# Gathering the rows of batches 4 to 7 in four groups between the stages of an embedding and attention kernel

## What is computed

```python
def _L0_tok_ref(token_ids, base_embeddings, rule_transform, token_rules):
    base_embeds = base_embeddings[token_ids]
    rule_indices = token_rules[token_ids]
    rule_matrices = rule_transform[rule_indices]
    return jnp.einsum('bsd,bsde->bse', base_embeds, rule_matrices)
...
h = _L0_tok_ref(x, L0_tok_base_embeddings, L0_tok_rule_transform, L0_tok_token_rules)
h = h + _L0_attn_ref(_layernorm(h, axis=-1), L0_attn_Q, L0_attn_K, L0_attn_VO)
h = h + _L0_ffn_ref(_layernorm(h, axis=-1), L0_ffn_Wg, ..., L0_ffn_b2)
```

## Time and profile before

| | us |
|---|---|
| median of 3 runs | 663.07 |
| lowest, highest | 662.15, 665.81 |
| the profiled execution | 663.97 |
| its span, first to last instruction | 662.2 |

### The profile page before, as it was taken

One profiled execution on the slowest core, in us unless ns is written; L12 is line 12 of the kernel. 1 busy time (PEld: TensorE's weight loads), 2 busy tenths in 40 slices (PEclk: granted clock), 3 DMA queues, 4 the chain that ended last, 5 costly groups with the idle time before them and its releaser, 6 DMA issues.

```text
span 662.2 us, 9427 instructions
## 1 busy us (share of the span) xinstructions
PE 526.7 (80%) x2732; PEld 291.5 (44%) x2732; DVE 419.1 (63%) x1018; ACT 288.0 (43%) x566; POOL 230.6 (35%) x379
## 2 busy tenths in 40 slices
PE   0173903697879379699999999999999899999684
PEld 0043801255644133344544554454454455666462
DVE  5621686563115166588868886896975866764566
ACT  0101401035554144445565556556555445466333
POOL 5674057623225710040134133223322413454422
PEclk9995965569799569799999999999999989999968
DMA  8732513813472106252422142044043100000000
GB/s 245 266 88 50 129 35 78 195 39 95 97 207 41 26 7 151 54 124 58 97 51 48 42 92 69 1 97 104 2 97 79 27 1 10 1 11 8 2 8 9
DMA packets 21935, 47.05 MB, mean 71 GB/s; under 512 B 6264, under 2 KB 11720, under 8 KB 21824
## 3 DMA queue, kind: packets, MB, share of 16 engines
q1 hardware_dynamic: 15552, 32.23, 20.5%
q0 software_dynamic: 4752, 8.20, 4.9%
q10 hardware_dynamic: 1584, 6.03, 2.8%
HBM read 9.97 MB, written 11.01 MB: 32 GB/s over the span
## 4 chain that ended last, share of the span: by engine, by line
PE 55%; DVE 18%; issue 9%; DMA 5%; another core or an unknown queue 4%; ACT 4%; POOL 3%; SPq 2%; DVEq 0%; ACTq 0%; POOLq 0%
PE bank L1217 13%; PE bank L1203 10%; PE bank L1183 6%; PE bank L1075 5%; PE bank L1145 4%; DVE mx L952 4%; PE bank L1167 4%; PE bank L1139 2%; PE bank L1140 2%; DVE r_sb L999 2%; POOL r_sb L586 1%; DMA front<-in_weights 1%; PE bank L1228 1%; POOL ctxT L517 1%
## 5 line engine op out<-in xcount | busy, mean ns | idle before, releaser
L952 DVE TENSOR_REDUCE mx<-bank 128x1 f32<-128x512 f32 x256 | 171.5, 687 | 111.1 <-PE bank L1203 84.4
L586 POOL TENSOR_TENSOR r_sb<-r_sb 128x256 f32<-128x256 f32 x180 | 93.9, 521 | 280.4 <-DVE r_sb L1017 176.6
L643 ACT ACTIVATE prob<-bank 128x512 f32<-128x512 f32 x256 | 139.0, 596 | 74.7 <-PE bank L1183 43.8
L1203 PE MATMUL bank<-ks,qs 96*128 96x512 f32 x256 | 124.7, 491 | 25.6 <-DVE mx L952 12.4
L1217 PE MATMUL bank<-prob,xa 128*64 128x512 f32 x448 | 125.3, 638 | 2.8 <-issue 2.8
L1203 PEld LDWEIGHTS bank<-ks,qs 96*128 96x128 f32 x256 | 51.4, 201 | 144.3 <-issue 122.9
L1183 PE MATMUL bank<-qs,ks 97*128 97x512 f32 x224 | 79.0, 435 | 0.8 <-DMA qs<-negm 0.8
L701 ACT ACTIVATE r_sb<-bank,stay 128x512 f32<-128x512 f32 x56 | 37.1, 687 | 44.9 <-PE bank L1140 44.6
L1075 PE MATMUL bank<-r_sb,eT 128*64 128x64 f32 (+1 forms) x544 | 44.4, 242 | 12.3 <-ACT eT L626 8.3
L1075 PEld LDWEIGHTS bank<-r_sb,eT 128*64 128x64 f32 x544 | 39.4, 154 | 19.6 <-issue 10.6
L1183 PEld LDWEIGHTS bank<-qs,ks 97*128 97x128 f32 x224 | 39.1, 196 | 16.8 <-issue 10.8
(11 more groups left out here) (159 smaller groups left out, 700.7 us busy)
## 6 DMA issues: line engine op xcount, KB each, us to landing
qs<-qk_h SPq DMA_DIRECT2D x64, 128.0 KB
ks<-qk_h SPq DMA_DIRECT2D x56, 128.0 KB
qs<-qk_l SPq DMA_DIRECT2D x32, 128.0 KB
ks<-qk_l SPq DMA_DIRECT2D x28, 128.0 KB
emb_sorted<-front ACTq DMA_DIRECT2D x4, 608.0 KB
y_sorted<-y_out POOLq DMA_DIRECT2D x19, 128.0 KB, 2.4
e_in<-emb_sorted POOLq DMA_DIRECT2D x9, 256.0 KB, 3.3
emb_sorted<-front ACTq DMA_DIRECT2D x3, 640.0 KB
```

Of the source, the lines that this page charges most:

```text
L586: nc.gpsimd.tensor_tensor(a[:, at:at + width], src[:, 0:width], src[:, width:2 * width], ALU.add).then_inc(S["pool_chain"], 1)
L643: nc.scalar.activation(prob[:, step % NPROB, u % 2, :], bank[u % NST][:], ACT.Exp, scale=SC).then_inc(S["exp_done"], 1)
L952: V.tensor_reduce(mx[:, u // 16, u % 16:u % 16 + 1], bank[3 + n % 2][:], AX.X, ALU.max).then_inc(S["mx_done"], 1)
L1203: M(bank[3 + n % 2][:], qs[0:96, nb % 2, h, tt * 128:(tt + 1) * 128], ks[0:96, nb % 2, h, :], start=True, stop=True).then_inc(S["s_ps"], 1)
```

## The change

Batches 2 and 3 are gathered where all six were. The rows of batches 4, 5, 6 and 7 are gathered at the start of stages 1, 2, 3 and 4, four transfers each, in front of the copy of values of that stage.

```diff
             for g in range(TOTAL - 4, TOTAL):
                 store_sent(pool, g)
-            for b in range(2, B):
-                bring(1, b)
+            bring(1, 2)
+            bring(1, 3)
             n = 0
...
             for b in range(-2, B + 1):
+                if 1 <= b and b + 3 < B:
+                    bring(1, b + 3)
                 if 2 <= b + 2 < B:
                     values(b + 2)
                 for k in range(16):
```

## The result

| | before | after | ratio of the two |
|---|---|---|---|
| median | 664.44 us, 4 runs (662.15 to 669.08) | 649.14 us, 4 runs (643.64 to 656.62) | 0.9731, interval 0.9678 to 0.9784 |
| profiled execution | 663.97 us (span 662.2) | 656.62 us (span 654.8) | |

The median fell by 15.3 us, where 12.6 was forecast from a median of before of 663.07. The profiled run of after is the slowest of its four and counts as slow, so the ratio leaves it out, and its whole span says little; it is read by stretches. (Lines after the change stand two lower: L952 is now L954, L1203 is L1205, L1217 is L1219, L1122 is L1124.)

What follows compares the result with a forecast made beforehand. DVE, ACT and PE were taken to stand idle on late words from PE during the row of 24 gathers. Gains 9.6 + 3 = 12.6 us; 663.97 - 12.6 = 651.4, median 0.9 lower: 650.5 us, range 643.5 to 661.

Steps and rivals of the forecast that it cites:

- The place and the mechanism: Row of 24 gathers: after some seven, PE's words to DVE and ACT come late, until at most 4 us after the last.
- The 9.6 us: Gain up to batch 2's transposes, starting at about 226 instead of 235.65, because the row ends at its eighth gather.
- both bouts: Two spells of late PE words beside the 24 gathers; the first, to 218.16, was expected to stay.
- nothing is late after 213.8: Upper end of the gain: transposes at 219.2 and the clock never falls; 19.9 us gained, so 643.3 us.
- The 3 us of clock: Gain from PE's clock, at half speed in 234 to 244, being up again at about 226; 3 us taken.
- the bound of 4.1: PE's 8.13 us of work in 234 to 244 would take 4.1 us at full clock; 3 of it was counted.
- What is late next: ACT's 6.68 us wait for stacking transfers before batch 3's projections moves forward whole, neither growing nor shrinking.
- The moved rows: Four rows of four gathers, 5.0 us of POOL each, fit its idle time with 4.7 us to spare; cost 0 us.
- The sum: Whole kernel: 9.6 + 3 = 12.6 us gained, 651.4 for the profiled execution, median 650.5 us.
- The rows crowd: Rival, chance 0.14: batch 4's row, soon behind the first eight gathers, brings its own stall of 7.5 us; 658 us.
- Every short row stalls PE: Rival, chance 0.07: each of the four moved rows costs 4.5 us; 668.5 us, or 682 with half clock.
- The gathers are only beside the stall: Rival, chance 0.13: something else at this place, such as instruction loading, holds the engines, or the stall recurs; 663 us.

Runs made afterwards that it cites:

- the row of 32: Against the changed kernel: batches 4 to 7 gathered in one row behind batch 2's value copy, plus 16 extra gathers; 673.99 us, ratio 1.0161 to the kernel before.

## Why the prediction was right, and where it was not

**The place and the mechanism** held on chips of the first kind. The late word from PE, the row as its cause and the release behind a short row were read from the rows of before, and the longer row at another place confirms them by making them worse there.

**The 9.6 us** were mis-sized. The step "they cleared 3 to 4 us after the last gather" and "I take 218.16 as it is. After it the step takes at most 5.78 us as at present" carried two waits of the long row over to the short one. Measured, the words were on time 1.7 us after the last of eight, there was no half clock, and the steps at 216.5 to 223.2 took 3.6 and 3.1 us. The transposes stood 16.7 us behind the first gather where 226 - 203.94 = 22.1 was forecast: 15.0 us gained instead of 9.6. Before, both bouts, but for the 1.1 us of their first slow step (3.24 against 2.15), belonged to the gathers behind the eighth; the bound in which "nothing is late after 213.8" (15.3 us to the transposes) was the nearer one, and its 19.9 us lies close to the 18.8 measured by the last subtraction.

**The 3 us of clock** were in the same way 3.8 (18.8 - 15.0): the clock never fell, and the whole of the bound of 4.1 was there to take.

**What is late next**: 6.65 us for the stacking transfers against 6.68, as forecast. **The moved rows** cost nothing: POOL has 4.73 us left where 4.7 was forecast, and no wait for a remote counter stands behind them.

**The sum** met the median (649.1 against 650.5) partly by luck, because errors cancel: the row gave 18.8 us, not 12.6, the profiled run of after lost some of it elsewhere, and the median of before came out 1.4 us above the one that the sum started from. The medians differ by 15.3 us, and the spread of the runs of after, 643.64 to 656.62, is wider than the term in question; where the 3.5 us between 18.8 and 15.3 went in the other three is not traced. The slowest of them, the profiled one, lost 6.8 us to the clock at 516 to 534; why it fell there no run tells.

**The rivals.** *The rows crowd* fell: batch 4's gathers at 224.46, 6.8 us behind the eighth, brought no bout (224 to 234: PE busy 9.93 of 10 us). *Every short row stalls PE* fell as well. *The gathers are only beside the stall* fell on the chips of the first kind, by the row of 32. One ground that was given for it, that the 24 scatters up to 124.26 went without a "remote" wait, was half right: the label is missing, but PE's words were late there too, by up to 3 us (the last section). The rule that PE and ACT never wait on anyone (the Trainium skill, "SBUF — State Buffer", "Who interferes with whom") doesn't cover what is seen: ACT idled 16.21 us before and 0.84 and 1.62 after, with nothing changed but the place of POOL's gathers. It speaks of ports of the memory, and what is late is a counter. The rule on instruction fetch (the Trainium skill, "Runtime: NRT & Kernel Launch", "Instruction fetch mechanics") would keep a stall at its place in the program; it moved with the row, so no run here shows it at work.

**What the prediction did not have** is that its premise could be false of the chip. That beside "the four gathers of batch 1" nothing was late was taken as a matter of the length of the row; on the other kind of chip 24 gathers went as harmlessly (traced on one, read from the time of the kernel before on two more). On those the result is the second rival's, no difference, and the 0.13 given to it rested on other grounds. The trace of before could not show it, as it came from one kind of chip. It could have shown one thing more: a wait of 2.57 us put down to "remote" at 23.59, beside an earlier row of 18 fetches, which the prediction does not count.

## What to carry to other kernels

Where DVE and ACT sit idle with "remote" as the releaser, on one core, and PE's work for them has long been done, look at what POOL issues: in some runs a long row of indirect transfers makes others wait up to 16 us for PE's counter updates (24 gathers in a row), where 8 gathers cost 1 to 3. The length is not all: beside 4 gathers and 24 scatters the words were up to 3 us late. What lies between 8 and 24 gathers was not tried; in the embedding part the one word beside the 18 fetches was 2 to 5 us late, and the latest beside the 8 scatters and 14 fetches 11 to 13 us. Issue only the transfers that are needed next, and put the others where the engine has a gap anyway; three gaps of 1 to 1.5 us, set by waits on PE's progress, brought 8 us in the embedding part, whereas a fixed pause before each transfer delayed the ones that are needed. And run the kernel before beside every experiment: a change of 2.3% on one chip was worth 0.0% on another.

## What the runs showed of the hardware

- **Two kinds of chips, or of moments.** The kernel before took 663 to 664 us (medians of 3 to 7 runs) on three occasions and 625.1, 625.6 and 625.3 us (19 to 25 runs each) on three others, each time on another chip. Nothing lay between: 660.5 to 669.1 us the ones, 622.8 to 632.8 the others, but for the one run of 2574. Of the difference 20.1 us stand behind the first gather of the row of 24, 15.8 of them before batch 2's transposes (31.7 - 15.9), and 20.0 ahead of it (203.9 - 183.9). As no chip was used on two occasions, it stays open whether the chip or the moment decides, and what it is.
- **PE's words are late, DVE's to PE are not.** With DVE idle 11.15 us for PE's word, PE took up DVE's answer 0.15 us after its end (234.25 + 0.69 to 235.09), and so it did after each of the four long waits of the row of 32 (238.73 + 0.69 to 239.57 is the first). PE had gone on past the matmul in question by then: four value matmuls were started at 223.94. The gathers themselves last 0.95 us on either kind of chip.
- **The lateness needs a run-up.** With eight gathers the waits came to 0.8 to 3.1 us at the very end; in the rows of 24 and 32 the long waits began 9 to 11 us after the first gather.
- **Not every long row costs the same.** The embedding part has two more. The first 18 fetches run from 4.71 to 28.43 us, and DVE's first wait for PE beside them reads, in before, in after, and in before on a chip of the second kind:

```profile
23.59 0.26 DVE L777 TENSOR_SCALAR cnt_i<-bank 128x100 int32<-128x100 f32 x1 [2.57 <-remote]
26.58 0.26 DVE L779 TENSOR_SCALAR cnt_i<-bank 128x100 int32<-128x100 f32 x1 [5.75 <-remote]
21.73 0.26 DVE L777 TENSOR_SCALAR cnt_i<-bank 128x100 int32<-128x100 f32 x1 [0.77 <-PE bank L1036]
```

  PE's last matmul for it ended at 21.68, 21.49 and 21.63 us, so the word was 1.9, 5.1 and 0.1 us late. The wait differs by 3.2 us between the first two, which is most of the 3.9 by which the embedding part of after ended later. And from 88.05 to 125.23 us POOL issues the 4 gathers of batch 0 and the 24 scatters, 28 indirect transfers with one copy among them. DVE's longest wait for a score tile there, in before, and the one wait as it recurs on a chip of the second kind:

```profile
126.84 0.69 DVE L952 TENSOR_REDUCE mx<-bank 128x1 f32<-128x512 f32 x1 [2.06 <-issue]
...
110.72 1.29 DVE L952 TENSOR_REDUCE mx<-bank 128x1 f32<-128x512 f32 x2 [0.35 <-PE bank L1203]
```

  The score tile for 126.84 is that of 124.81, which took 0.77 us, so the word was some 1.3 us late; in after the latest of this stretch is 2.9 us behind its tile (126.05 + 0.77 to 129.69). Beside the 8 scatters and 14 fetches the word for the second copy of y_out was 12.7 us late in before (48.12 + 1.15 to 62.01) and 11.1 in after (51.95 + 1.97 to 65.00), and in the row of 24 gathers DVE's was 10.2 us late (223.24 + 0.77 to 234.25). Whether it matters that these are scatters, or what PE does beside them, no run tells.
